# The two states of a pair laid end to end across a PSUM bank boundary: a scan of 1000 columns in place of 1012

## The reference, cut to what matters

```
xi = conv(in_proj(x));  xc = silu(xi + conv_b)
dt, Bm, Cm = split(x_proj(xc))
delta = softplus(dt_w(dt) + dt_b)
A = -exp(A_log)
h[t] = exp(delta[t] * A) * h[t-1] + delta[t] * Bm[t] * xc[t]      # per channel d and state n, h[-1] = 0
y[t] = sum over n of h[t] * Cm[t]
y = (y + xc * Dv) * silu(z);  out = out_proj(y)
f + b halved, added to x, layer norm, residual, layer norm
```

## Time and profile before

| what | value |
|---|---|
| median of 3 runs | 3269.98 us (3268.59 to 3270.75) |
| the profiled execution, its own time | 3269.01 us |
| its span in the trace | 3267.2 us |
| busy: DVE, ACT, POOL, PE | 93%, 92%, 90%, 90% |
| granted TensorE clock, mean | 0.971 |

### The profile page before, as it was taken

One profiled execution on the slowest core, in us unless ns is written; L12 is line 12 of the kernel. 1 busy time (PEld: TensorE's weight loads), 2 busy tenths in 40 slices (PEclk: granted clock), 3 DMA queues, 4 the chain that ended last, 5 costly groups with the idle time before them and its releaser, 6 DMA issues.

```text
span 3267.2 us, 53223 instructions
## 1 busy us (share of the span) xinstructions
PE 2929.2 (90%) x18304; PEld 2225.0 (68%) x18304; DVE 3031.7 (93%) x2455; ACT 3006.6 (92%) x5633; POOL 2943.1 (90%) x1829
## 2 busy tenths in 40 slices
PE   5899898999899998999999999999989988999985
PEld 3776766776767766667667677677667666676664
DVE  4999999999999999999999999999999999999995
ACT  4999999999999999999999999999999999999994
POOL 2889999999999999999999999999999999999996
PEclk9999999999999999999999999999999999999997
DMA  2223222232322232222222222322222322222221
GB/s 76 94 83 95 93 90 87 81 97 93 96 91 88 80 97 91 91 92 84 95 91 92 90 91 83 97 91 92 91 91 83 97 91 91 91 82 94 90 87 45
DMA packets 102208, 290.53 MB, mean 89 GB/s; under 512 B 11371, under 2 KB 36150, under 8 KB 101942
## 3 DMA queue, kind: packets, MB, share of 16 engines
q1 hardware_dynamic: 101942, 287.12, 27.7%
HBM read 276.84 MB, written 10.24 MB: 88 GB/s over the span
## 4 chain that ended last, share of the span: by engine, by line
PE 42%; ACT 23%; DVE 12%; POOL 11%; issue 11%; SPq 0%; DVEq 0%; DMA 0%; POOLq 0%; ACTq 0%
PE y_ps L331 13%; POOL hc L819 9%; ACT da L677 8%; PE m_ps L364 6%; ACT w L623 6%; DVE hc L931 6%; PE g_ps L331 6%; PE m_ps L373 4%; PE m_ps L426 4%; DVE g_ps L918 3%; ACT L664 3%; PE m_ps L380 2%; PE m_ps L387 2%; PE g_ps L450 2%; PE g_ps L451 2%
## 5 line engine op out<-in xcount | busy, mean ns | idle before, releaser
L819 POOL TENSOR_TENSOR hc<-hc,c_all 128x1000 f32<-128x1000 f32 x1024 | 2346.3, 2311 | 225.1 <-DVE hc L931 210.7
L931 DVE TENSOR_TENSOR_SCAN hc<-da,g_ps 128x1012 f32<-128x1012 f32 x1024 | 2270.3, 2250 | 127.7 <-PE g_ps L331 58.1
L677 ACT ACTIVATE da<-delta,a_neg 128x498 f32<-128x498 f32 x2048 | 1330.9, 698 | 5.8 <-DVE hc L931 5.0
L331 PEld LDWEIGHTS y_ps<-ident,hc 128*125 128x125 f32 x8192 | 1044.0, 194 | 299.4 <-issue 183.3
L331 PE MATMUL y_ps<-ident,hc 128*125 128x128 f32 x8192 | 1115.2, 281 | 42.1 <-POOL hc L819 42.0
L623 ACT ACTIVATE w<-ut,bt 125x256 f32<-125x256 f32 x2048 | 891.8, 496 | 0.5
L331 PE MATMUL g_ps<-ident,w 125*128 125x125 f32 x4096 | 569.6, 285 | 226.1 <-DVE hc L931 219.3
L331 PEld LDWEIGHTS g_ps<-ident,w 125*128 125x128 f32 x4096 | 467.1, 147 | 277.0 <-DVE hc L931 264.5
L918 DVE TENSOR_TENSOR g_ps<-u,g_ps 128x1000 f32<-128x1000 f32 x512 | 608.5, 1188 | 42.7 <-PE g_ps L451 42.0
L364 PE MATMUL m_ps<-zt,convw 128*128 128x500 f32 x1024 | 473.3, 584 | 0.7 <-ACT zt L560 0.7
L364 PEld LDWEIGHTS m_ps<-zt,convw 128*128 128x128 f32 x1024 | 189.0, 190 | 151.8 <-issue 120.7
(11 more groups left out here) (59 smaller groups left out, 2133.6 us busy)
## 6 DMA issues: line engine op xcount, KB each, us to landing
c_all<-c_rows SPq DMA_DIRECT2D x512, 500.0 KB, 3.6
xin<-x_t SPq DMA_DIRECT2D x32, 375.0 KB, 7.6
out<-out_sb SPq DMA_DIRECT2D x32, 250.0 KB
c_rows<-dbl SPq DMA_DIRECT2D x64, 31.2 KB, 1.6
c_all<-f_conv_w SPq DMA_DIRECT2D x1, 512.0 KB
c_all<-b_conv_w SPq DMA_DIRECT2D x1, 512.0 KB
hc<-f_in_w SPq DMA_DIRECT2D x1, 128.0 KB
inw<-f_in_w SPq DMA_DIRECT2D x1, 128.0 KB
```

The source lines that it names most:

```text
L331: return pe.matmul(dst, src, ident[0:rows, 0:rows], start=first, stop=last, is_transpose=True, skip_group_check=True)
L677: op = act.activation(states(da[n % RING])[j].rearrange("p (s t) -> p s t", s=SC)[:, :, 1:T], steps, ACT.Exp, scale=a_neg[:, p % 2, db, 2 ...
L819: pool.tensor_tensor(hc, hc, c_all[:, pair % CRING], ALU.mult).then_inc(hc_ready, 1)
L931: dve.tensor_tensor_scan(h[n % HRING][:, 0:UC], da[n % RING][:], g_ps[n % 2][:, 0:UC], 0.0, ALU.mult, ALU.add).then_inc(scanned, 1)
```

## The change

The two states now lie end to end. In `da` and `h` they take columns 0 to 499 and 500 to 999 of tiles of 1000 columns. In `g_ps` they take columns 12 to 511 of the first bank and 0 to 499 of the second, so that they meet at the boundary of the banks and each matmul still writes into one bank. The scan covers 1000 columns. POOL's product is written as one run of 1000 columns on all its operands. The two instructions that cleared the gap in `g_ps` are gone. The number and the order of all other instructions on every engine stay as they were.

```diff
-UC = BANK + TC
+LEAD = BANK - TC
...
-        da = [sb(f"da{j}", [128, UC]) for j in range(RING)]
-        h = [sb(f"hc{j}", [128, 2 * BANK]) for j in range(HRING)]
+        da = [sb(f"da{j}", [128, 2 * TC]) for j in range(RING)]
+        h = [sb(f"hc{j}", [128, 2 * TC]) for j in range(HRING)]
...
-            return tile[:, 0:TC], tile[:, BANK:UC]
+            return tile[:, 0:TC], tile[:, TC:2 * TC]
+
+        def across(g):
+            return g[:, LEAD:LEAD + 2 * TC]
...
-        def paired(tile):
-            return tile[:, 0:2 * BANK].rearrange("p (n t) -> p n t", n=2)[:, :, 0:TC]
...
-                            at = e * BANK + j * TP
+                            at = LEAD + e * TC + j * TP
...
-                    pe.matmul(g[:, 0:TC], pick[:, 2 * r, :], upper(dbl[p % 2][0:K2, :]), start=True, stop=True)
-                    pe.matmul(g[:, BANK:UC], pick[:, 2 * r + 1, :], upper(dbl[p % 2][0:K2, :]),
+                    pe.matmul(g[:, LEAD:BANK], pick[:, 2 * r, :], upper(dbl[p % 2][0:K2, :]), start=True, stop=True)
+                    pe.matmul(g[:, BANK:BANK + TC], pick[:, 2 * r + 1, :], upper(dbl[p % 2][0:K2, :]),
...
-                hc = paired(h[n % HRING])
-                pool.tensor_tensor(hc, hc, c_all[:, pair % CRING], ALU.mult).then_inc(hc_ready, 1)
+                hc = h[n % HRING][:]
+                pool.tensor_tensor(hc, hc, c_all[:, pair % CRING].rearrange("p n t -> p (n t)"), ALU.mult).then_inc(hc_ready, 1)
...
-            for j in range(2):
-                dve.memset(g_ps[j][:, TC:BANK], 0.0).then_inc(setup_dve, 1)
...
-                g = paired(g_ps[n % 2])
+                g = across(g_ps[n % 2]).rearrange("p (n t) -> p n t", n=2)
...
-                dve.tensor_tensor_scan(h[n % HRING][:, 0:UC], da[n % RING][:], g_ps[n % 2][:, 0:UC], 0.0,
+                dve.tensor_tensor_scan(h[n % HRING][:], da[n % RING][:], across(g_ps[n % 2]), 0.0,
```

More of the change, by code:

```diff
@@ L245, in audio_tower_kernel @@
         LOADED = 16 * len(loads)
-        SETUP_DVE = 1 + RING + 2 + 1 + 1 + 2 * TAPS + 1 + 4
+        SETUP_DVE = 1 + RING + 1 + 1 + 2 * TAPS + 1 + 4
         def states(tile):
-            return tile[:, 0:TC], tile[:, BANK:UC]
+            return tile[:, 0:TC], tile[:, TC:2 * TC]
+        def across(g):
+            return g[:, LEAD:LEAD + 2 * TC]
         def upper(tile):
             return tile.bitcast(BF16).rearrange("p (t two) -> p t two", two=2)[:, :, 1]
-        def paired(tile):
-            return tile[:, 0:2 * BANK].rearrange("p (n t) -> p n t", n=2)[:, :, 0:TC]
         def wait_drained(eng, *j):
```

## The result

The changed kernel takes 3260.13 us (median of 7 runs, 3258.59 to 3264.14), the kernel before took 3271.03 beside it (7 runs, 3268.59 to 3271.64). The ratio is 0.9968, with a 95% interval of 0.9957 to 0.9980: 10.9 us less; the interval ends at the 0.2% that can be told from no change. The forecast was 6.3 us less, 3263.7.

The account below looks back on a forecast made before the run. The prediction took a ring of stretches of ACT, PE, DVE and POOL as the bound: 8 scans x 25.4 ns = 0.203 us a period, 6.3 us over 31 periods, all else 0; 3269.98 - 6.3 = 3263.7 us, range 3250 to 3269.

Parts of the forecast that it names:

- The ring: Stretches of ACT, PE, DVE and POOL, each the late engine in turn, set the 99.3 us period; only scans there count.
- Eight scans: DVE's scans of backward steps 6, 7, 13, 14, 15 and forward 0, 1, 2; 0.203 us a period.
- The price of a column: DVE's scan: 2.11 ns a column, so 25.4 ns for 12 columns; bounds 12.9 and 26.7 ns.
- The layout at nothing: POOL's product as one run, PE's fills, `times_b` and ACT's decays at new start columns: taken as 0.
- Both rivals on POOL's product: Product up to 179 ns shorter (3247 us, chance 0.08) or longer from its new place (3280 us, 0.07).
- All of it arrives: Rival: DVE's back-to-back queue is the bound, so all 26.0 us go: 3244.0 us; chance 0.10.
- F belongs to POOL and PE: Rival: POOL's products and PE's addition set the pace there; three scans count, 2.4 us, 3267.6 us; chance 0.20.
- F: DVE's stretch, 1635.93 to 1655.37: statistics, scans 13 to 15, next pass's steps 0 to 2; gives up 0.15 us.
- What is late next: DVE's three waits grow 0.6 us in all; ACT's gate wait of 1.32 shortens by 0.15.
- that wait of 1.32: ACT's wait for the gates at the end of F, counted as cover larger than the 0.15 us given up.
- the triple of DVE waits: DVE's waits in a period: 0.31 before backward step 6, 0.53 before step 12's statistics, 1.74 before forward scan 15.
- the wait of 1.74: DVE's wait in us before the scan of forward step 15, for PE's fill; expected to grow towards 2.0.

Follow-up runs that it names:

- lead_all_1012: States end to end as in the changed kernel, but each scan covers 1012 columns again, 12 cleared ones in front; 3269.49 us beside 3270.51 of before.
- rest_1000: Against the kernel before, the 24 scans of a period off the ring cover 1000 columns, the eight on it still 1012; 3266.91 us, ratio 0.9991.
- ring_1000: Against the kernel before, only the eight scans on the ring cover 1000 columns, the other 24 of a period 1012; 3261.73 us, ratio 0.9973.
- fills_twice: Changed kernel with four fills of `g_ps` a period issued twice on PE, with the same result; 3256.62 us, ratio 0.9961.
- stats13: Changed kernel with DVE's statistics of the last normalisation behind the scan of step 13, not 12, of the backward pass; 3261.3 us, ratio 0.9973.
- stats13_fills_twice: Changed kernel with DVE's output statistics one step later (13) and four fills of `g_ps` a period issued twice; 3256.5 us, ratio 0.9962.
- tail14: Changed kernel with the first half of the output projection at step 14, not 13, of the forward pass; 3256.89 us, ratio 0.9965.
- stats13_tail14: Changed kernel with both moves: output statistics behind backward step 13, first half of the output projection at forward step 14; 3258.52 us, ratio 0.9965.
- before_stats13: Kernel before (scans of 1012) with DVE's output statistics behind step 13, not 12, of the backward pass; 3259.52 us, ratio 0.9968.

## Why the prediction was right

- **The ring** was right. Eight scans give 0.18 to 0.19 us a period, 24 give 0.01 to 0.02; predicted were 0.203 and 0. The sum of the periods is 6.3 to 6.6 us against 6.3. What the measured 0.22 has beyond the eight may be a little of scan 3, whose end set PE's fill for step 5 by 0.03 us in the kernel before; that is read from the trace and wasn't tried.
- **The price of a column** was right: 25 ns for 12 columns (2250 to 2225), against 25.4, and the same again upward to 1024. Twice the product's rate, 25.8, is 0.8 above it, so the half throughput that the Trainium skill (DVE: opcode table, instruction layouts, handler registers and perf-mode slots, section 6, Datapath and trigger behaviour) gives for the built-in scan agrees with these rows to some 3%.
- **The layout at nothing**, POOL's runs included, was right: `lead_all_1012`, and 2311 against 2312 ns. Both rivals on POOL's product fall, and with them the estimate from the Trainium skill (GPSIMD Engine Reference, section 7, Performance pitfalls for Q7 kernels) of 85 ns saved a product.
- **All of it arrives** falls by `rest_1000`; **F belongs to POOL and PE** falls for the changed kernel by `ring_1000`, where six of the eight scans are F's. With the statistics moved, DVE isn't late there any more, and ACT's gate wait is at its floor.
- **What is late next**: the waits grew by 0.17, 0.15 and 0.20 (predicted: 0.6 in all), the gate wait shrank by 0.17 (0.15). But the text counted that wait of 1.32 as cover. Its last 0.69 us is a floor, so the cover was 0.63, still enough for 0.15.
- **The reading of the periods** was off. The prediction says that 27 of 32 have the triple of DVE waits with the same sizes; the trace has the wait of 1.74 (within 0.03) in 22, and all three in 18. Its period of 99.3 is a mean that has the disturbed ones in it; the usual one is 99.17. The sum uses neither number.
- **The step that was missing** is a term for the disturbed periods. The prediction took the first and the last together as one, and the others that differ as usual ones, without asking why they differ. Most of it is stretches of PE at 1.2 GHz, and when they fall elsewhere, start, disturbed periods and tail together move by microseconds: 1.4 more than before in one execution of the changed kernel, 4.3 less in another. As both are the same kernel, this part isn't the change's alone. The measured 10.9 is the ring's 6.3 to 6.6 and this; the periods bear out the forecast of 6.3, and the other 4.3 us are nothing that it foresaw. For the seven runs behind the median it was not traced; it is read from two executions, and in `rest_1000` from a third.

Why the stretches fall where they do stays open. In `fills_twice`, with more work on PE in four places, none falls in the forward pass from the third period on; in `stats13`, with one step moved on DVE, they do in nearly all.

The lowest medians are those of `stats13_fills_twice`, `fills_twice` and `tail14` (3256.5, 3256.6 and 3256.9 us), 0.9962, 0.9961 and 0.9965 of before; their intervals overlap the changed kernel's, so none is clear of it. What is left to win shows in the free periods of `stats13_tail14`, 0.9 us below the changed kernel's; no run here keeps the stretches away and leaves F free.

## What to carry to other kernels

Where four engines are all about 90% busy, follow the waits around one period as a ring: only work in the stretches where its own engine is the late one counts, and making the other work longer, up to its wait, is nearly free (24 scans with 12 columns more cost 0.01 to 0.02 us a period here). Before counting a wait as slack look for its floor, the same wait in a place where nothing else is late; and most of a wait that is off the ring comes back elsewhere when it is taken away. A change of some tenths of a per cent needs the periods read one by one, since the granted clock in a few of them can move as much time as the change. Take the mark on the ring: by a mark beside it the periods with and without a stretch can't be told apart.

## What the runs showed of the hardware

- A DVE scan of f32 costs 25 ns for 12 columns between 1000 and 1012, and the same again to 1024 (2275), with one operand in PSUM. An operand in PSUM may run across the boundary of two banks; whether the two states meet there or lie 12 columns apart makes no difference (2250 ns in the kernel before and in `lead_all_1012`). No run here has a scan within one bank.
- TensorE's granted clock falls from 2.4 to 1.2 GHz for some 3 us one to three times in 99 us, in a kernel whose PE is 90% busy, also after windows in which PE shows no idle time, and it stayed up after windows in which PE idled half the time. Matmul rows of 1.02 us take 1.73 there. In the forward pass one costs 0.5 us a period in `stats13` and 0.7 in `before_stats13`; the tail without one at step 12 of the last forward pass is 2.3 us shorter; about 84 us after the token copy it costs nothing.
- POOL's product of 1000 columns takes the same time over two runs of 500 and over one of 1000 (2311 and 2312 ns).
